# Cross-attention with layer norm: the last two blocks reordered on TensorE, VectorE and GpSimd, and mask rows held on SyncE until the row maxima have landed

## What is computed

```python
q, k, v = heads(x @ W_Q.T), heads(ctx @ W_K.T), heads(ctx @ W_V.T)
scores = einsum('bhqd,bhkd->bhqk', q, k) / sqrt(16)
scores = where(mask[:, None] == 1, -1e9, scores)
p = softmax(scores, axis=-1)
out = concat_heads(einsum('bhqk,bhkd->bhqd', p, v)) @ W_O.T + x
mu, var = mean(out, -1), mean((out - mu) ** 2, -1)
return (out - mu) * rsqrt(var + 1e-5) * gamma + beta
```

## Time and profile before

| what | value |
|---|---|
| median of 3 runs | 176.94 us (175.6 to 178.7) |
| the profiled execution | 177.09 us |
| its span | 175.3 us, so 1.79 us lie around it |
| mean granted TensorE clock | 0.971 |
| TensorE busy | 152.7 us (87%) |
| VectorE busy | 139.5 us (80%) |
| GpSimd busy | 96.0 us (55%) |
| ScalarE busy | 105.1 us (60%) |

### The profile page before, as it was taken

One profiled execution on the slowest core, in us unless ns is written; L12 is line 12 of the kernel. 1 busy time (PEld: TensorE's weight loads), 2 busy tenths in 40 slices (PEclk: granted clock), 3 DMA queues, 4 the chain that ended last, 5 costly groups with the idle time before them and its releaser, 6 DMA issues.

```text
span 175.3 us, 3587 instructions
## 1 busy us (share of the span) xinstructions
PE 152.7 (87%) x1264; PEld 82.4 (47%) x1264; DVE 139.5 (80%) x308; ACT 105.1 (60%) x140; POOL 96.0 (55%) x125
## 2 busy tenths in 40 slices
PE   7699939887969999999999999998899798799840
PEld 7456515344335356345545544563456363164530
DVE  0967743569399969998999899899989975759894
ACT  3123224355377883888877897778576559796400
POOL 8300430010564525337767977974744785899890
PEclk9999985899999999999999999999999999999996
DMA  5959868764867997887498877749460023011206
GB/s 157 382 142 135 242 101 258 230 161 103 268 172 196 286 292 184 222 277 168 137 236 234 247 200 178 214 162 228 133 223 5 0 120 123 2 64 60 120 0 239
DMA packets 21909, 30.24 MB, mean 173 GB/s; under 512 B 3436, under 2 KB 17436, under 8 KB 21892
## 3 DMA queue, kind: packets, MB, share of 16 engines
q1 hardware_dynamic: 20340, 28.18, 56.4%
q10 hardware_dynamic: 1552, 1.84, 3.8%
HBM read 11.28 MB, written 4.19 MB: 88 GB/s over the span
## 4 chain that ended last, share of the span: by engine, by line
PE 51%; DVE 19%; DMA 10%; issue 9%; ACT 5%; POOL 2%; ACTq 1%; SPq 0%; DVEq 0%; POOLq 0%
PE pv_ps L993 12%; PE scores_ps L984 9%; DVE neg_max L725 7%; PE max_ps L951 6%; PE work_ps L924 6%; PE work_ps L930 5%; PE scores_ps L930 4%; DMA R<-neg_max_t 4%; DMA x_t<-in_x_cols 4%; DVE ctx_q L733 3%; PE work_ps L1012 3%; DMA R<-first_max_t 3%; ACT probs L594 2%; PE work_ps L1009 2%; ACT neg_max_t L584 1%
## 5 line engine op out<-in xcount | busy, mean ns | idle before, releaser
L594 ACT ACTIVATE probs<-scores_ps 78x1024 f32<-78x1024 f32 x60 | 60.5, 1016 | 24.4 <-PE scores_ps L984 19.6
L725 DVE TENSOR_REDUCE neg_max<-max_ps 128x6 f16<-128x462 f32 (+1 forms) x84 | 44.7, 560 | 5.2 <-PE max_ps L951 5.1
L951 PEld LDWEIGHTS max_ps<-kb,R 125*128 125x128 f16 x512 | 26.4, 99 | 36.9 <-DVE neg_max L725 21.0
L409 POOL TENSOR_TENSOR ctx_n<-ctx_q,rden 128x256 f32<-128x256 f32 x31 | 19.8, 639 | 43.0 <-DVE rden L735 42.9
L984 PE MATMUL scores_ps<-R,kb 127*78 127x512 f16 x120 | 37.0, 392 | 2.3 <-DMA R<-first_max_t 2.0
L951 PE MATMUL max_ps<-kb,R 125*128 125x77 f16 x512 | 32.5, 201 | 6.1 <-DVE neg_max L725 5.5
L993 PE MATMUL pv_ps<-probs,v_all 78*32 78x512 f32 x248 | 33.0, 604 | 2.6 <-ACT probs L594 1.5
L733 DVE STREAM_TRANSPOSE ctx_q<-pv_ps 128x512 f32<-128x512 f32 x31 | 21.8, 704 | 4.6 <-PE pv_ps L993 4.4
L430 POOL TENSOR_TENSOR y<-y,gamma_sb 128x512 f32<-128x512 f32 x14 | 17.8, 1276 | 2.4 <-ACT y L599 2.4
L392 POOL TENSOR_SCALAR eq<-mask_i 77x512 f16<-77x512 int32 x3 | 5.8, 1928 | 22.1 <-DMA mask_i<-in_mask_cols 22.1
L599 ACT ACTIVATE y<-y,shift,rstd 128x256 f32<-128x256 f32 x28 | 15.1, 591 | 3.6 <-POOL shift L423 3.6
(11 more groups left out here) (105 smaller groups left out, 198.7 us busy)
## 6 DMA issues: line engine op xcount, KB each, us to landing
R<-eq SPq DMA_DIRECT2D x12, 616.0 KB
R<-q SPq DMA_DIRECT2D x46, 128.0 KB
x_t<-in_x_cols SPq DMA_DIRECT2D x8, 512.0 KB, 5.9
y<-in_x SPq DMA_DIRECT2D x8, 512.0 KB, 6.0
out<-y SPq DMA_DIRECT2D x7, 512.0 KB, 2.7
mask_i<-in_mask_cols SPq DMA_DIRECT2D x8, 154.0 KB
out<-y ACTq DMA_DIRECT2D x2, 256.0 KB, 2.1
kb<-k SPq DMA_DIRECT2D x10, 39.0 KB, 3.2
```

Source lines behind the costliest of these rows:

```text
L409: nc.gpsimd.tensor_tensor(ctx_n[:, v, :, u * DK:(u + 1) * DK], ctx_q[:, t % 2, :, 0:DK], rden[:, t % 2, :].unsqueeze(2).to_broadcast([P, C ...
L594: nc.scalar.activation(probs[:, s, :, :], scores_ps[scores_buffer(PAIRS * n + s)[0]][0:COLS, :, :], ACT.Exp).then_inc(exp_done, 1)
L725: nc.vector.tensor_reduce(to[:, t, lo:hi], max_ps[u % 2][:, 0:(hi - lo) * KEYS].rearrange("p (h k) -> p h k", k=KEYS), AX.X, ALU.max, nega ...
L951: last = nc.tensor.matmul(max_ps[u % 2][:, (h - lo) * KEYS:(h - lo + 1) * KEYS], R[m % R_RING][0:MAX_ROW, h, t * P:(t + 1) * P], kb[0:MAX_ ...
```

## The change

Four edits, and one semaphore less.

- SyncE: the first half of the q rows of block n+3 is issued ahead of its mask rows; between them SyncE waits until the maxima of block n+1 have landed (`s_nm`). This is in turns n = 0 to 4.
- VectorE: in block 6 both `stats` of block 4 stand at step 3. The addition of beta on VectorE (block 5, second half) is gone, and its semaphore with it.
- GpSimd: it takes that addition over, behind `norm(7, 2)`. For each half, the pow of the last block stands ahead of the addition of beta of block 6.
- TensorE, block 7: `scores(7, 6)` ahead of `project_out(6, 1)`, `scores(7, 7)` ahead of `values(7, 2)`, and `last_out(0, t)` with `last_residual(t)` behind `last_values`.

```diff
             def store_y(m):
-                if m == N - 3:
-                    sp.wait_ge(beta_last, 1)
-                    sp.wait_ge(y_beta, 2 * m + 1)
-                elif m == N - 2:
-                    sp.wait_ge(y_beta, 2 * m + 1)
-                else:
-                    sp.wait_ge(y_beta, 2 * (m + 1))
+                sp.wait_ge(y_beta, 2 * (m + 1))
...
                 if n + 3 < N:
+                    load_q(n + 3, 0)
+                    sp.wait_ge(s_nm, 16 * (n + 1))
                     load_mask(n + 3, 0)
-                    load_q(n + 3, 0)
...
             norm(N - 1, 2)
+            plus_beta(N - 3, 1)
 
             for half in range(2):
                 times_gamma(N - 2, half)
             for half in range(2):
-                plus_beta(N - 2, half)
                 two = slice(2 * half, 2 * half + 2)
                 pool.wait_ge(last_ve, half + 1)
                 nc.gpsimd.tensor_tensor(rstd_last[:, two], var_eps_last[:, two], minus_half[:, two], ALU.pow).then_inc(last_rstd, 1)
+                plus_beta(N - 2, half)
...
-                    if s in ((1, 3) if n == N - 2 else (3, 5)) and n >= 2:
-                        stats(n - 2, int(s == (3 if n == N - 2 else 5)))
+                    if n == N - 2 and s == 3:
+                        stats(n - 2, 0)
+                        stats(n - 2, 1)
+                    elif s in (3, 5) and 2 <= n < N - 2:
+                        stats(n - 2, s // 2 - 1)
...
             turn(n, 2)
-            plus_beta(n - 2, 1)
             for half in range(2):
                 turn_last(half)
...
             scores(n, 5)
+            scores(n, 6)
             pe.wait_ge(out_ready, 2 * (n - 1) + 1)
             project_out(n - 1, 1)
-            scores(n, 6)
+            scores(n, 7)
             values(n, 2)
-            scores(n, 7)
...
-            last_out(0, 0)
-            last_out(0, 1)
             pe.wait_ge(exp_done, PAIRS * N)
             pe.wait_ge(pv_turned, QUADS * n + QUADS - 1)
             last_values(0)
             last_values(1)
-            last_residual(0)
-            last_residual(1)
+            for t in range(2):
+                last_out(0, t)
+                last_residual(t)
```

More of the change, by code:

```diff
@@ L233, in cross_attention @@
         ve_ready, rstd_ready, shift_ready = sem("ve_ready"), sem("rstd_ready"), sem("shift_ready")
-        y_normed, y_gamma, y_beta, beta_last = sem("y_normed"), sem("y_gamma"), sem("y_beta"), sem("beta_last")
+        y_normed, y_gamma, y_beta = sem("y_normed"), sem("y_gamma"), sem("y_beta")
         ident_ready, last_scaled, last_shifted = sem("ident_ready"), sem("last_scaled"), sem("last_shifted")
@@ L759, in stats @@
                     nc.vector.bn_aggr(mean_var[:, m % 2, t, :], bn[:, m % 2, t, :]).then_inc(mv_ready, 1)
[L761 to L764, removed]
             def turn_last(half):
```

## The result

The changed kernel takes 185.51 us (median of 4 runs, 184.63 to 185.93) against 177.21 us before: ratio 1.049, 95% interval 1.044 to 1.054. It is slower by 8.3 us where 0.8 us less was forecast, and lies far outside the range of 174.5 to 178.2. The profiled execution took 184.63 us, with a span of 182.8 against 175.3. Runs of one kernel here spread over up to 7 us; the ratios leave disturbed runs out.

A forecast was written before the change was run, and what follows sets the result against it. TensorE (87% busy) was taken to bound the kernel, with gaps waiting on VectorE's reductions and the maxima's DMA; -0.77 - 0.45 + 0 + 0 + 0.4 = -0.8 us, from 177.09 to 176.3, range 174.5 to 178.2.

The forecast's parts named there:

- Part 1, statistics: Block 6: a reduction 0.77 us earlier closes nearly all of TensorE's 0.85 us gap; taken as -0.77 us.
- Part 2, what the hold removes: Start of block 2: with masks held, the maxima land some 3 us earlier and the scores' wait goes; -0.45 us.
- first rival: The hold gives nothing: maxima are slow through q rows and loads, which stay; 176.7 us, chance 0.17.
- The second: Rival: stores don't collide, or maxima stalled more in ordinary runs than in the profiled one; 174.9 us, chance 0.18.
- Part 2, what the hold adds: SyncE's queue behind the held masks: q rows land at about 92, before ScalarE's copy at 93.33; taken as 0.
- third rival: Slower: q rows land late, q copy waits, TensorE stops, up to 1 us in turns 1 to 3; 179.1, chance 0.13.
- its list of what would show it wrong: q copy waiting for DMAs at step 4 of blocks 2 to 4, second mask half late, or last exponential unmoved.
- The slack of 1 us: Turn 2: about 1 us between the q rows landing at about 92 and ScalarE's q copy at 93.33.
- the slower case: The third rival: maxima still taking 5 to 5.6 us, q rows landing at about 93.5 to 94.5; 179.1 us, chance 0.13.
- The weighing of the rule: Maxima DMA: by the queue rule the hold gives nothing, by the profile row 0.45 us; the forecast took the row.
- Part 3, TensorE in block 7: Last exponential about 0.9 us earlier, but last values wait for VectorE's third turn, gaining 0.1; counted as 0.
- Parts 4 and 5, the tail: VectorE ends 0.5 us earlier, but block 6's 512 KB store goes out between block 7's halves and collides; +0.4 us.

The follow-up runs named there:

- e7: Kernel before with only the statistics edit, both statistics of block 4 at step 3 of block 6: ratio 1.0060 (1.0009 to 1.0111).
- e12: The same kernel as e7, timed longer: ratio 0.9995 (0.9947 to 1.0042).
- e5: Changed kernel with two q16 buffers, so ScalarE's q copy waits for the rows of two blocks before, not one: ratio 1.028 (1.019 to 1.037).
- e13: As e9, with three eq16 buffers on top: median 177.00 us against 176.61 for the kernel before, no ratio.
- e2: Changed kernel with SyncE's queue as before, so all edits but the hold: ratio 0.9954 (0.9908 to 0.9999).
- e16: The same kernel as e9, timed longer: ratio 1.0057 (1.0007 to 1.0108).
- e9: Changed kernel with two q16 buffers and, in turns 1 and 2, loads of mask words and transposed x ahead of the hold: 179.04 us against 176.38, no ratio.
- e8: As e7, plus GpSimd's pow of the last block ahead of the addition of beta of block 6: ratio 1.005 (1.000 to 1.011).
- e14: Kernel before with both statistics at step 3, pow ahead of beta, and the store of block 6 in two 256 KB halves: ratio 0.9954 (0.9902 to 1.0007).
- e1: Kernel before with SyncE's edit alone (q rows ahead of mask rows, wait for the maxima between): ratio 1.036 (1.026 to 1.047).
- e4: Kernel before with the wait for the maxima ahead of both mask rows and q rows, order as before: ratio 1.058 (1.043 to 1.072).

## Why the prediction was wrong, point by point

**Part 1, statistics (-0.77): right in the trace.** The gap went, and the interval shrank by 0.85, in all profiles that have the edit. No timing shows it (e7 and e12).

**Part 2, what the hold removes (-0.45): not borne out.** In the changed kernel the maxima's DMAs are shorter (median 3.2 against 3.8, the longest 5.1 against 6.5) and the wait at block 2 is gone, but there they are issued late, behind the stalled q copy, while the traffic drains. Where the hold stays and the q copies are on time, they take 6.5 us (e5) and 6.6 us (e13), as before, and in e13 the scores wait 0.43 us again. The step that failed is "with 616 KB of masks out of the way it lands some 3 us earlier": with the masks out of the way the q rows and loads issued from 52 to 62 us still kept the engines busy (share 0.95 to 1.02 from 58 to 66 us in e5). That is the prediction's first rival. The second has something for it too: without the hold the scores waited 2.1 us in e2 and 2.8 us in e12 for the maxima, against 0.3 in the profile that the prediction read.

**Part 2, what the hold adds (0): this is the step that failed.** The prediction named the right mechanism and the right victim in its third rival, q rows too late for the q copy and TensorE stopped, and its list of what would show it wrong is what the trace shows. It gave it a chance of 0.13 and 0.8 us for each turn. Four things in its working were wrong:

- *The q rows' landing.* It was worked out as mask bytes, then q bytes, in turn at 190 GB/s: 8.5 us of transfer, and "landed at about 92", 9.4 us behind the end of the hold at 82.6. Measured: 13.75 in turn 1 (67.40 to 81.15) and 11.6 in the turn that was priced (86.45 to 98.1). The rate was near enough, 184 GB/s from 67.40 to 81.15; but that is 2.5 MB, and masks and q rows are 1.6 MB, so 0.9 MB of other transfers moved in that time, and since the engines had stood nearly idle from 66 us to the end of the hold, they were ones issued behind it. SyncE needed 1.9 us for each of two q issues, and the last q DMA landed 6.65 us behind its issue, with 512 KB loads issued behind it in flight. A transfer's landing in a full queue wasn't its place in line divided by the rate.
- *The turn that was priced.* The slack of 1 us was read from one turn, the one where maxima are issued at 79.11, and taken for all. That turn had the smallest of the stalls, 1.15 us of ScalarE's waiting; its neighbours had 4.17, 3.41 and 3.19. The worst came first, where three 512 KB loads and those of gamma and beta stand behind the same q rows; no run tested whether they made the difference.
- *The clock.* A stall was priced as its own length. Behind two of the three long gaps TensorE ran at half its clock for several us, and the interval with the gap of 2.87 us grew by 4.80.
- *One victim.* Only the q copy was followed. Everything behind a waiting instruction in SyncE's queue is late: with q16's reuse out of the way 2.8% of loss were left (e5), with the load of x too 0.6% (e16). A third reader, TensorE's own maximum units over R, shows in the profile of e9 only (VectorE's comparison waits there too, beside it).

So the slower case needed no maxima of 5 to 5.6 us: in turns 2 and 3, with landings of 3.2 and 3.5 us, it came as well.

**The weighing of the rule.** The Trainium skill ("DMA: Bandwidth & Descriptors", section on queues, rings and completion order) has each DMA engine go round its queues packet by packet. The prediction drew two things from it: that the masks would hardly hold up the maxima, and that holding them gives nothing. On the second the traces agree: 6.5 and 6.6 us with the masks held (e5, e13), 6.5 without. But a 16 KB DMA on ScalarE's queue still took 6.5 us beside SyncE's other traffic against 2.1 alone, so its own queue did not keep it clear of that traffic.

**Part 3, TensorE in block 7 (0): right.** From turn 7 to the last values 18.83 instead of 19.00; the last values start when VectorE's third turn is done, as forecast.

**Parts 4 and 5, the tail (+0.4): right in sum, +0.55, wrong in one step.** VectorE ends 0.6 earlier behind the last values, and the collision of three stores costs more than that (e8 and e14 show the collision by itself). But VectorE's 0.6 doesn't come from the first small addition, which still took 0.80 at 173.84, with GpSimd's second gamma beside it until 174.62. It comes from the multiplication at 171.97, 0.29 instead of about 0.8: it now starts just ahead of GpSimd's gamma, not inside it.

**The sum.** Without the hold the forecast of the parts is -0.77 + 0 + 0.4 = -0.4 us, 0.998; e2 measured 0.995 (0.991 to 1.000). So nearly the whole of the miss is the term "I take 0" for the q rows behind the held masks, where SyncE's edit cost 8 us and more; the -0.45 that was not there is small beside it.

## What to carry to other kernels

A wait put into the queue of an engine that issues DMAs holds everything behind it. Before pricing it at nothing, list each transfer behind it with its reader and the reader's slack in every turn, not in one. Don't take bytes over rate for a landing in a full queue: the time to issue and the transfers behind it count as well. If the forecast rests on a slack of 1 us in a loop, the case where it is gone deserves more than one chance in eight, and its price must count what TensorE's clock may do after a gap. Before clearing the way for a transfer, look at how much its readers really wait for it, in more than one profile: here 0.3 us before and 2.8 us in e12. And a transfer that got shorter after a change may only have been issued later: count from what makes its data, not from its issue.

## What the runs showed of the hardware that was not expected

- Issuing a 128 KB DMA of q rows from SyncE took 0.6 us with little outstanding (77.03 after) and up to 2.1 us right behind 1.2 MB of masks (110.08 after). The queue itself becomes a place to wait.
- DMAs of one queue didn't land in proportion to their place: a 128 KB transfer landed 6.65 us after its issue, and 0.9 MB more than stood in front of it and in it moved from the end of the hold to its landing.
- A 16 KB DMA on ScalarE's queue took 2.1 us alone and 6.5 to 6.6 us beside SyncE's loads and q rows, with masks held (e5, e13) or not (before).
- TensorE's granted clock fell to 0.50 behind gaps of 2.87 and 1.93 us after and of 1.67 in e1, and not behind 2.41 after or 2.15, 2.28 and 1.86 in e4. In e8 and e14 the same instructions with the same gaps of 1.0 and 0.4 us were followed by 1.00 in one and 0.50 in the other. The length of the gap alone did not decide it.
- VectorE's addition on 128 x 2 elements took 0.17 us with GpSimd idle (e8) and 0.80 us when it started inside a 128 x 512 operation of GpSimd (before, after, e7), ending with it.
